# A graph layer on one core: 60 blocks selected by one-hots in place of 52, the first at step 9 of 196 in place of 7

## The reference

```python
j_idx, i_idx = edge_index[0], edge_index[1]
x_j, x_i = x[j_idx], x[i_idx]
msg = jnp.concatenate([x_i, x_j - x_i], axis=-1)
h = jax.nn.relu(msg @ W1 + b1)          # 64 -> 64
h = jax.nn.relu(h @ W2 + b2)            # 64 -> 128
h = jax.nn.relu(h @ W3 + b3)            # 128 -> 64
m = h @ W4 + b4                         # 64 -> 32
s = jax.ops.segment_sum(m, i_idx, num_segments=N_NODES)
cnt = jax.ops.segment_sum(jnp.ones((m.shape[0],), m.dtype), i_idx, num_segments=N_NODES)
x = _layernorm(x + s / jnp.maximum(cnt, 1.0)[:, None], axis=-1)
```

## Time and profile before

| | us |
|---|---|
| runs | 1564.91, 1569.15, 1566.78 |
| median | 1566.78 |
| span of the profiled execution | 2441.1 |

### The profile page before, as it was taken

One profiled execution on the slowest core, in us unless ns is written; L12 is line 12 of the kernel. 1 busy time (PEld: TensorE's weight loads), 2 busy tenths in 40 slices (PEclk: granted clock), 3 DMA queues, 4 the chain that ended last, 5 costly groups with the idle time before them and its releaser, 6 DMA issues.

```text
span 2441.1 us, 39243 instructions
## 1 busy us (share of the span) xinstructions
PE 1767.5 (72%) x13131; PEld 1040.0 (43%) x13131; DVE 947.9 (39%) x3086; ACT 602.6 (25%) x945; POOL 1125.9 (46%) x1165
## 2 busy tenths in 40 slices
PE   3133777777768777878787778786867778777797
PEld 2112444444444444444444444444444444444454
DVE  3663343333333343333333333443333333333356
ACT  2233122222212222212222222222221222122234
POOL 5275444453544454354545454544444454444411
PEclk7555787877878787777778877777877877787888
DMA  5334643343434443353434353544344344444332
GB/s 128 98 93 88 200 112 112 106 140 94 136 101 116 126 121 109 103 147 91 135 105 136 104 152 92 152 109 114 104 123 115 111 114 109 133 118 118 109 106 59
DMA packets 189929, 283.06 MB, mean 116 GB/s; under 512 B 84614, under 2 KB 90169, under 8 KB 189156
## 3 DMA queue, kind: packets, MB, share of 16 engines
q1 hardware_dynamic: 152341, 241.67, 33.7%
q0 software_dynamic: 36704, 37.00, 7.3%
q10 hardware_dynamic: 682, 1.85, 0.3%
HBM read 266.51 MB, written 13.73 MB: 115 GB/s over the span
## 4 chain that ended last, share of the span: by engine, by line
PE 63%; issue 23%; another core or an unknown queue 6%; DVE 3%; ACT 2%; DMA 1%; SPq 1%; DVEq 0%; POOL 0%; ACTq 0%; POOLq 0%
PE ps L964 22%; PE ps L996 12%; PE ps L988 10%; PE ps L1019 5%; PE ps L1004 4%; PE ps L919 3%; PE ps L901 3%; PE ps L1016 2%; PE ps L978 2%; ACT work L716 1%; ACT work L731 1%; DMA sums<-in_src 1%; DVE region L1410 0%; DVE region L1292 0%
## 5 line engine op out<-in xcount | busy, mean ns | idle before, releaser
L585 POOL DMA_INDIRECT xj<-z_rows,src_t x1107 | 1074.5, 971 | 1190.9 <-PE ps L919 787.7
L964 PE MATMUL ps<-region,x_p 128*96 128x150 bf16 (+53 forms) x5876 | 569.6, 243 | 416.6 <-issue 407.2
L964 PEld LDWEIGHTS ps<-region,x_p 128*96 128x96 bf16 x5876 | 440.6, 142 | 572.9 <-issue 566.7
L731 ACT ACTIVATE work<-ps,b3s 128x512 f32<-128x512 f32 x196 | 134.7, 687 | 1335.5 <-PE ps L996 1037.1
L996 PE MATMUL ps<-work,w3s 128*64 128x512 f32 x784 | 356.6, 840 | 21.2 <-issue 21.1
L1377 DVE TENSOR_SCALAR region<-region,cst 128x1565 bf16<-128x1565 int16 (+6 forms) x416 | 245.7, 634 | 268.0 <-remote 256.3
L988 PE MATMUL ps<-work,w2s 64*128 64x512 f32 x784 | 298.1, 827 | 6.8 <-ACT work L716 5.6
L724 ACT ACTIVATE work<-ps,b2s 128x512 f32<-128x512 f32 x392 | 250.7, 684 | 161.0 <-PE ps L988 82.7
L1392 DVE COPY work<-ps 128x512 f32<-128x512 f32 x194 | 133.4, 687 | 336.4 <-PE ps L1004 217.0
L1386 DVE CAST work<-ps 96x512 bf16<-96x512 f32 x52 | 35.7, 686 | 513.9 <-PE ps L964 506.8
L1410 DVE TENSOR_SCALAR region<-iota_g,dst_rel 128x42 f32<-128x42 f32 x1120 | 185.7, 250 | 0.0
(11 more groups left out here) (156 smaller groups left out, 826.3 us busy)
## 6 DMA issues: line engine op xcount, KB each, us to landing
dstb<-dst_rows SPq DMA_DIRECT2D x196, 252.0 KB
region<-src_rows SPq DMA_DIRECT2D x104, 391.2 KB
region<-src_rows SPq DMA_DIRECT2D x52, 407.2 KB
region<-src_rows SPq DMA_DIRECT2D x52, 403.2 KB
region<-src_rows SPq DMA_DIRECT2D x52, 376.2 KB
region<-src_rows SPq DMA_DIRECT2D x52, 375.8 KB
region<-src_rows SPq DMA_DIRECT2D x52, 374.0 KB
region<-src_rows SPq DMA_DIRECT2D x52, 366.2 KB
```

The costliest lines, as they stand in the source:

```text
L585: pool.indirect_dma_start(out=xj[:, u, j % UT, j // UT, 0:w], out_offset=None, in_=rows, in_offset=bass.IndirectOffsetOnAxis(ap=cols[:, j: ...
L964: chosen = nc.tensor.matmul(ps[0:XP, XBANK[h], lo - h * UE:hi - h * UE], xb[:, a, :], hot[:, q % QN, at + lo:at + hi], start=not begun[h], ...
```

## The change

Sixty blocks are sorted and selected in place of 52, and the first stands at step 9 in place of 7. From `SB` follow all counts: the gathered blocks go from 144 to 136, the gathers from 1147 to 1083, the tiles that hold one row for a sorted block from 52 to 60 partitions. `SORTED_AT` is now 9, 12, 15 and so on up to 188, with a distance of 3 but for two of 4; before, of the 51 distances 23 were 3 and 28 were 4.

```diff
-SB = 52
+SB = 60
 HALVES = 64
 GB = S_N - SB
 B0 = SB * PE2
...
 AHEAD = 4
 HALF_STEP, PARTS_STEP = 0, 1
-FIRST_SORTED, LAST_SORTED = AHEAD + 3, S_N - 8
+FIRST_SORTED, LAST_SORTED = AHEAD + 5, S_N - 8
 SORTED_AT = [FIRST_SORTED + k * (LAST_SORTED - FIRST_SORTED) // (SB - 1) for k in range(SB)]
```

## The result

The changed kernel takes 1575.75 us (median of eight runs, 1571.69 to 1576.51), the kernel before, run beside it, 1567.80. The ratio is 1.0051, interval 1.0038 to 1.0063: **slower by 0.5%**, where 1527 us was forecast.

A forecast was written before the change was run, and what follows sets the result against it. POOL was taken to bound before; 80.0 us less gathering would leave it at 1486.8, so PE would bound: 1472.6 + 54.0 = 1526.6 us, forecast as 1527, range 1515 to 1545, eight in ten 1488 to 1595.

The forecast's parts named there:

- Part (a): On POOL: eight blocks fewer gathered, 64 gathers at 1.25 us, 80.0 us off, leaving POOL's path at 1486.8 us.
- POOL's sum: Before the change: loop begin 205.4 + gathers 1313.8 + landing 4.1 + end 41.0 = 1564.3 us, 2.5 under the median.
- Rival 4: In POOL's gathers: DVE's fast operations stretch them, at most 180 us; at pitch 1.30 POOL needs 1533.6 us; chance 0.06.
- Part (d): On DVE: each added block's eight builds, second pick and cast fit into 7 us of slack per period; cost nothing.
- Part (b): On PE: eight more selected blocks at 6.75 us each, 54 us, making PE's path 1526.6 us.
- POOL keeps its lead to the end: In the ring of ten blocks: per three steps PE needs 20.25 us, POOL 20.0, so gathers stay ahead.
- Rivals 1, 2 and 3: Selection dearer beside other work, 1601.6 us, chance 0.16; long matmul trains slower, 1665 us, 0.02; PE already bounding, 1612 us, 0.07.
- the late triple: Three steps near the stretched profile's end, PE busy throughout, 20.25 us, taken as what an undisturbed run does.
- rival 5: POOL stays the bound, PE being cheaper than thought: 1486.8 us; chance 0.09.
- Part (c): Before the first selection: moving the start from step 7 to 9 spares PE a wait, worth 0 to 9 us.
- Part (e): In the DMA queues: added window loads, 15.9 of 20.25 us per period, cost nothing, but with a thinner margin.
- What would show it: Signs: longer profiled span, late triple at 20.25 us; wrong if mean gather over 1.0 us or time above 1567.

The follow-up runs named there:

- e7: The changed kernel with the builds' source numbers laid out in three rows with gaps between them; 1468.48 us, ratio 0.9375 to the kernel before.
- after: The changed kernel as profiled: 60 blocks, the first at step 9, against the kernel before; 1575.75 us, ratio 1.0051.
- before, again: The kernel before, rerun with nothing changed, for a trace that is not stretched; 1566.34 us, ratio 1.0005.
- e5: The changed kernel with builds comparing two SBUF sources in place of one source and a scalar; 1664.01 us, ratio 1.0628 to the kernel before.
- e3: The kernel before with only the later start: 52 blocks, the first at step 9; 1567.38 us, ratio 1.0010.
- e6: The changed kernel with 56 blocks in place of 60, the first at step 9; 1570.89 us, ratio 1.0034 to the kernel before.
- e2: The kernel before with only the new count: 60 blocks, the first at step 7; 1567.94 us, ratio 1.0021.
- e4: The changed kernel with two builds per step placed between the one-hots of destinations; 1570.12 us, ratio 1.0025 to the kernel before.
- e8: The changed kernel with the builds' source numbers laid out in four rows with gaps; 1578.26 us, ratio 1.0057 to the kernel before.
- e10: The changed kernel with source numbers in three rows and the first block at step 7; 1469.68 us, ratio 0.9392 to the kernel before.

## Why the prediction was wrong

**The direction was wrong, by the price of a gather.** Part (a) took 1.25 us as the pitch of all gathers and so 80.0 us off POOL. The kernel before already had 1.296, and the changed one has (1530.19 - 154.51) / 986 = 1.395. The step that made 1.25 look right was the agreement of POOL's sum with the median, "with no term fitted": its loop begin was 50 us too late (205.44 for 155.11, both it and the pass count from the stretched trace) and its pitch 0.046 us x 1050 = 48 us too low. The two errors nearly cancelled, and the sum came within 2.5 us of the median by luck; it was taken as a proof.

**Rival 4 was the mechanism, at a wrong size.** It took 0.3 us for an operation from the earlier trace rows and bounded 60 blocks at 180 us, then took 0.03 us a gather from the mean of the stretched trace, 971 ns, and priced the rival at a pitch of 1.30 us, with a chance of 0.06. But in that trace POOL waited 787.7 us for PE, so gathers and builds met in another way than undisturbed. The real 144.4 us (142.6 of it beside builds and picks, the operations that the rival named) lies near the bound and far from the choice; the earlier trace rows, the one row that showed the clash itself, should have weighed more than a mean over meetings that the stretching had thinned out.

**Part (d), DVE at nothing, failed with it.** DVE had the slack (e7 uses 183 us more of it and is faster). But its time was not only its own: what an added build costs is what it takes from POOL.

**Part (b) and the step prices were right.** 6780 matmuls of L964, no wait for builds (0.3 us), and periods of 20.25 us, in after's windows with PE busy throughout:

```profile
core 0: us, PE busy (x) PEld busy (x) DVE busy (x) ACT busy (x) POOL busy (x), PEclk, DMA share, GB/s
400.00:420.25 20.25, 20.25 (x221) 13.89 (x219) 13.19 (x46) 8.18 (x13) 15.99 (x14) 1.00 0.74 228
...
1000.00:1020.25 20.25, 17.41 (x153) 12.60 (x150) 11.64 (x41) 5.86 (x9) 15.77 (x15) 0.79 0.63 187
```

PE runs so until about 600 us. Then the lead of the ten blocks is used up: a period takes 16 gathers, POOL issues 14 in it, and PE waits, as at 1000 us, where the granted clock also averages 0.79, a part of the stretch at the lower of its two levels. The statement that "POOL keeps its lead to the end" fell. Where PE does bound, its path comes out, in e7's timeline of layer 2 (step 4's, and step 195's):

```profile
149.02 2.08 PE L993 MATMUL ps<-work,w2s 64*128 64x512 f32 x4
...
1428.22 1.13 PE L993 MATMUL ps<-work,w2s 64*128 64x512 f32 x4
```

From the end of the one, 151.1, to the end of the other, 1429.35, are 1278.3 us; the prediction's prices give 191 x 4.50 + 60 x 6.75 = 1264.5, and 10 of the 13.8 between them lie before step 9. What was wrong in its 1526.6 was the loop's begin, 226.7 for 151.1. Rivals 1, 2 and 3 are thereby out, and the late triple was a true measure of PE's steps, although the prediction had said that a time above 1567 would mean the contrary; rival 5 had the bound right (POOL) and the price not.

**Part (c)** asked for the wait before the first selection, and it indeed went, from 6.77 us in before, again, to none; the first selection starts at 163.11, after step 6, as forecast. The wait moved to step 8, whose destination numbers SP loads only behind the eight stores and the window loads, as far as after's timeline shows:

```profile
148.22 6.30 SPq L482 DMA_DIRECT2D src_rows<-region  x8
...
157.45 4.41 SPq L491 DMA_DIRECT2D region<-src_rows  x8
...
173.67 0.48 DVE L1369 TENSOR_SCALAR region<-dstb,node_off 126x1024 bf16<-126x1024 int16 x1 [7.89 <-DMA dstb<-dst_rows]
...
174.30 0.64 PE L901 MATMUL ps<-region,ywin 126*64 126x512 bf16 x2 [5.54 <-DVE region L1369]
```

**Part (e)** was right: builds wait 1.8 us for loads in all. **"What would show it"** named a mean gather over 1.0 us as the sign of an error, and it is 1.089; the guess that the profiled span would grow with the instructions was wrong, since the stretching was that one execution's.

**What stays open.** In each undisturbed period of 20.25 us the number of gathers locks: 14 in 23 of 27 periods of after, 13 in 18 of 20 of e5, 16 in all 53 of e7; before, again, alternates between 15 and 16. That the old kernel's mixed distances of three and four steps break the lock and keep its price at 1 us a block fits e3 and e6, but count and distances changed together, and a version with 60 blocks at broken distances was not tried. The starts point the same way, for at equal distances the same meeting comes again in every period, but they do not show what sets the moment. Why the lock falls on 14 and not on 15 is not explained, nor why a gather that begins just before a train lasts to its end and one that begins just after does not.

## What to carry to other kernels

An engine with slack is not free: ask what it shares with the engine that bounds, and price its fast operations by the row in which the two meet. A slower mode on the idle engine can be the faster kernel; here 0.37 us more a build bought 107 us. And a sum that meets the median is no proof when its terms come from a disturbed execution: check one of them, such as the loop's begin, against the time that the rest leaves.

## What the runs showed that was not expected

- A gather that begins some 0.15 us before a train of three builds can last until 0.8 us after the whole train, 2.65 us beside one of 1.68 and 3.67 beside one of 2.69. One that begins 0.1 to 0.3 us after the train's begin takes 1.25 us and ends within it (after and before, again).
- An operation with two inputs in SBUF holds up a gather just as a fast one does (e5, mean 1171 ns).
- A source laid out in three rows gives builds of 1009 ns for 637, and gathers of 0.94 us beside them; one in four rows changes neither.
- The excess per block was 1.0 us at mixed distances and 2.4 at nearly equal ones, where POOL issues the same 14 gathers in 23 of 27 periods. That the regularity is the cause is not shown.
- A store of 58 rows takes SP 18.69 us for eight, where eight of 60 take 6.25 to 6.51 (after, e2, e4, e5, e7, e8, e10).
